# Products made two groups ahead of an engine's other steps, in the local stage of a four-block model

## The reference

```python
x = x + attn_a(layernorm(x))   # local: 16 heads of 16, each query sees 44 fixed offsets
x = x + ffn(layernorm(x))      # 8 groups of 512 tokens, two linear maps, no activation
x = x + attn_b(layernorm(x))   # full attention over 2 x 2048 tokens, rotary q and k
x = x + ffn(layernorm(x))
```

```python
k_mod = k[:, :, idx] * (1.0 + scale_embed)            # idx = t - offset, 0..40, 128, 96, 384
scores = einsum('bhtd,bhtjd->bhtj', q, k_mod) / sqrt(HD) + pos_bias    # masked where idx < 0
attn = softmax(scores)
out = einsum('bhtj,bhtjd->bhtd', attn, v[:, :, idx]) * if_gain
```

## Time and profile before

| | us |
|---|---|
| median of 3 runs | 2927.61 |
| lowest and highest | 2920.57, 2934.63 |
| the profiled execution | 2935.33 |
| its span | 2933.7 |

### The profile page before, as it was taken

The page is one execution under the profiler, slowest core; times in us unless marked ns, Lnnn a source line. Parts: engine busy times, 40 slices in busy tenths (PEclk is TensorE's granted clock), DMA queues, the critical chain, the costliest instruction groups (busy, mean ns, idle before and its releaser), DMA issues. The chain is left out here.

```text
span 2933.7 us, 50620 instructions
## 1 busy us (share of the span) xinstructions
PE 2547.2 (87%) x15600; PEld 1009.9 (34%) x15600; DVE 2106.6 (72%) x3525; ACT 1382.5 (47%) x1695; POOL 736.7 (25%) x971
## 2 busy tenths in 40 slices
PE   7678788788887756799899899898999999999787
PEld 5334444444443431233232233232233333323233
DVE  4376767767777536588788788788888888888323
ACT  0133333333333310466566566566666666666611
POOL 0487655656665202400200201002000000000000
PEclk9799899989998885899999999999999999999999
DMA  7324434334334326900400402204000000000042
GB/s 229 115 61 109 112 88 120 95 98 127 79 102 126 99 75 98 100 7 15 54 7 19 50 4 40 29 7 61 4 15 11 8 19 8 7 19 7 22 157 97
DMA packets 243735, 183.54 MB, mean 63 GB/s; under 512 B 103172, under 2 KB 212373, under 8 KB 243605
## 3 DMA queue, kind: packets, MB, share of 16 engines
q1 hardware_dynamic: 209366, 115.80, 14.7%
q0 software_dynamic: 15936, 45.64, 9.4%
q10 hardware_dynamic: 18306, 20.59, 2.2%
HBM read 120.44 MB, written 52.77 MB: 59 GB/s over the span
## 5 line engine op out<-in xcount | busy, mean ns | idle before, releaser
L1172 DVE TENSOR_REDUCE mx<-ps_m 128x1 f32<-128x512 f32 x2064 | 1301.1, 683 | 285.4 <-PE ps_m L1034 276.8
L1158 ACT ACTIVATE pr<-ps_s 128x1024 f32<-128x1024 f32 x1024 | 995.1, 1021 | 604.4 <-PE ps_s L1092 604.0
L1034 PE MATMUL ps_m<-ks,qs 96*128 (+1 forms) x2064 | 723.0, 393 | 46.9 <-DMA qs<-q_d 28.2
L1092 PE MATMUL ps_s<-qs,ks 99*128 (+1 forms) x2048 | 616.2, 382 | 62.1 <-POOLq L968 29.2
L1062 PE MATMUL ps_o<-pr,vg 128*32 128x512 f32 x4104 | 551.2, 609 | 0.6 <-ACT pr L1158 0.6
L515 POOL TENSOR_TENSOR prod_p<-qT,kT 128x512 f32<-128x512 f32 x336 | 412.8, 1259 | 53.6 <-ACT qT L700 22.8
L1034 PEld LDWEIGHTS ps_m<-ks,qs 96*128 (+1 forms) x2064 | 162.3, 97 | 653.6 <-DVE mx L1172 306.9
L978 POOL DMA_DIRECT2D o_d<-on x34 | 18.7, 551 | 1289.4 <-DVE on L1182 1252.1
L1092 PEld LDWEIGHTS ps_s<-qs,ks 99*128 (+1 forms) x2048 | 196.3, 98 | 307.4 <-issue 91.2
L559 PE MATMUL PSa<-prod_p,sj 128*32 128x512 f32 x672 | 211.5, 633 | 71.1 <-ACT sc L712 28.3
L559 PE MATMUL PSa<-prod_d,sj 128*32 128x512 f32 x736 | 211.6, 630 | 69.2 <-DVE prod_d L768 37.8
(11 more groups left out here) (140 smaller groups left out, 2312.7 us busy)
## 6 DMA issues: line engine op xcount, KB each, us to landing
own<-skew SPq DMA_DIRECT2D x64, 512.0 KB
ks<-k_d POOLq DMA_DIRECT2D x42, 256.0 KB, 8.9
qs<-q_d POOLq DMA_DIRECT2D x168, 64.0 KB, 8.9
skew<-attn SPq DMA_DIRECT2D x64, 164.0 KB, 4.3
o_d<-on POOLq DMA_DIRECT2D x34, 256.0 KB, 2.3
w<-in_W SPq DMA_DIRECT2D x8, 1024.0 KB
w<-in_W2T SPq DMA_DIRECT2D x8, 1024.0 KB
vb_d<-vb SPq DMA_DIRECT2D x8, 1024.0 KB, 4.4
```

The lines of the kernel that those rows point to most:

```text
L1034: pe.matmul(ps_m[:, pos % 3, :], qs[0:KROWS, bass.ds(nq, 1), j, qt * P:(qt + 1) * P].rearrange("p a t -> p (a t)"), ks[0:KROWS, bass.ds(ns ...
L1092: mm = pe.matmul(ps_s[:, pair, jj, :], ks[:, bass.ds(slot, 1), j, kk * P:(kk + 1) * P].rearrange("p a t -> p (a t)"), qs[:, bass.ds(q, 1), ...
L1158: act.activation(pr[:, kk % 2, 2 * pair:2 * pair + 2, :], ps_s[:, pair, :, :], ACT.Exp, scale=HD ** -0.5).then_inc(p_ready, 1)
L1172: return dve.tensor_reduce(mx[:, j * TILES + qt, kc:kc + 1], ps_m[:, pos % 3, :], AX_X, ALU.max).then_inc(m_read, 1)
```

## The change

VectorE and GpSimd make, in slot s, the products of slot s+2 (`LEAD`), and then take the slot's other steps; VectorE's wait for constants moves to slot -2 with them. TensorE still takes the products of slot s in slot s, but in every fourth slot, where a new bank begins, it does its other steps first. The first "q" of a chunk moves one slot forward. The rings stay at 6.

```diff
+LEAD = 2
-    (-7, "h_normalise", 0), (-6, "k", 0), (-5, "k", 1), (-3, "q", 0), (1, "v", 0), (3, "v", 1), (6, "q", 1),
+    (-7, "h_normalise", 0), (-6, "k", 0), (-5, "k", 1), (-4, "q", 0), (1, "v", 0), (3, "v", 1), (6, "q", 1),
...
@@ GpSimd
-                if 0 <= slot < NG * SLOTS:
-                    products(slot // SLOTS, slot % SLOTS)
+                if 0 <= slot + LEAD < NG * SLOTS:
+                    products((slot + LEAD) // SLOTS, (slot + LEAD) % SLOTS)
...
@@ TensorE
-                if 0 <= slot < NG * SLOTS:
+                late = slot % 4 == 0
+                if 0 <= slot < NG * SLOTS and not late:
                     products(slot // SLOTS, slot % SLOTS)
                 for j, what, i in steps_in(slot):
                     step(j, what, i)
+                if 0 <= slot < NG * SLOTS and late:
+                    products(slot // SLOTS, slot % SLOTS)
...
@@ VectorE
-                if slot == 0:
+                if slot == -LEAD:
                     dve.wait_ge(filled, 6)
                     dve.wait_ge(const_ld, 16 * N_CONST)
-                if 0 <= slot < NG * SLOTS:
-                    products(slot // SLOTS, slot % SLOTS)
+                if 0 <= slot + LEAD < NG * SLOTS:
+                    products((slot + LEAD) // SLOTS, (slot + LEAD) % SLOTS)
```

## The result

| | before | after |
|---|---|---|
| median of 7 runs, us | 2927.84 | 2949.41 |
| lowest and highest | 2920.57, 2934.63 | 2940.96, 2952.96 |
| span of the profiled execution | 2933.7 | 2947.8 |
| its mean granted clock | 0.930 | 0.929 |

The ratio is 1.0063, 95% interval 1.0049 to 1.0076: the changed kernel is slower by 0.6%, some 18 us (21.6 by the medians). I had forecast 2911 us, 0.6% faster. The time lies at the upper end of the range, the sign is wrong, and the price is that of the rival "the ring behind the late slot 16" (2945 us).

A forecast was written before the change was run, and what follows sets the result against it. No engine is full in the local stage; TensorE's waits for VectorE and ScalarE bound it. Six periods of 3.5 gained less 1.6 lost, plus 5 in the fill, give 16.4 us off 2927.6: 2911 us, range 2870 to 2950.

The forecast's parts named there:

- the ring behind the late slot 16: Slot 16: VectorE waits for score matmuls put behind "h_back" and two "values"; slower, 2945 us; chance 0.16.
- What bounds the stage: Local stage, 128 to 968 us: no engine is full; TensorE's waits before its score matmuls, together 137 us, are the target.
- Half A: Chunk from "k" to the end of "qk", 76.2 us before: 3.5 us gained, ends 1 and 6.
- Half B: Chunk from the end of "qk" to the next "k", 39.8 us before: 1.6 us lost, ends 1.2 gained and 4.7 lost.
- GpSimd's burst: Half B, six GpSimd products in a row, 8.27 us, slowing VectorE's operations beside them; 1.0 us taken as freed.
- put on the rival: Clock rival: fewer but longer TensorE waits, each followed by 6.8 us more at half clock; slower, 2952 us; chance 0.08.
- my end of 4.7: From "qk" to the next "k": the losing end, 4.7 us lost, with "k" at values + 20.6.
- The rule of shared ports: VectorE with two SBUF inputs and GpSimd reading SBUF exclude each other for a whole instruction; up to 1.3 us each.
- The fill: From 128 to 256 us, where GpSimd sets the pace: 5 us gained, between 0 and 14.
- The sum: Whole kernel: (3.5 - 1.6) x 6 + 5 = 16.4 us gained; the tail after slot 192 has no products.
- The signs: Right: no score bank wait, new "pv" and "turn" waits, period near 114 us; wrong: period under 110 or over 117.
- threshold: Slot 16's products first used later than about 10.9 us after "values" starts (9.0 + 1.9 net) decides the sign.

## Why the prediction was wrong

**What bounds the stage.** That was read rightly: the waits of the earlier trace rows went, and the period is set by TensorE meeting VectorE. It held so well that the regular chunk did not move at all.

**Half A.** Forecast 3.5 us gained, ends 1 and 6; measured 76.2 - 71.6 = 4.6. The half clock after slot 4's update is gone as forecast, and "pv" waits for the mask add: 2.6, 1.7 and 2.0 us in slots 20, 5 and 8, where I had 2.4, 1.2 and 1.6. Before "turn" it waits 0.5 and 0.2 us in slots 3 and 9, where I had 1.4 and 1.9; that is most of what half A gained over the forecast. After the last "pv" of these of them stands a new 3.4 us at half clock (558.8), half of what I had feared for the lower end.

**Half B, the positions.** Forecast: "values" at qk + 23.9, VectorE's held product 9.0 us later, by its terms the mask add ended at values + 14.2 (9.0 + 0.6 + 2.8 + 1.25 + 0.55), "k" at values + 17.5. Measured: 595.73 - 570.30 = 25.4; 8.8; 14.0; 18.9. The mechanism was told rightly down to the instruction, and two terms were mis-sized. The first is the 1.0 us taken as freed from GpSimd's burst: nothing was freed, since a GpSimd that is held by its ring starts its burst later and not never, and it fell beside the next operations of the same kind. I had asked where GpSimd would stop, not where it would go on. The second is the clock: TensorE's wait of 4.62 us (I had 3.3) is followed by 3.3 us with a granted clock of 0.52, close to its lower level of 1.2 GHz, which I had put on the rival and not into the sum. Together half B lost 4.5 us where I had 1.6, near my end of 4.7.

**The rule of shared ports.** I weighed the Trainium skill (SBUF — State Buffer, "SBUF: two separate sides"), by which the two engines exclude each other for a whole instruction, and gave a freed operation up to one product. In the regular chunk the trace agrees, with 1.46 and 1.76 us. In the fill it does not stop at one: 6.33 us, until five products of GpSimd had passed. The measurement decides, and in the fill this is worth some 4 us that I had not in the sum.

**The fill.** Forecast 5 us gained, between 0 and 14; measured, from the first product to the copy of chunk 2's "k", 9.4 us lost. This is the step that failed most, and its range had no side below zero. The argument "GpSimd sets the pace, so little comes back" treated a lead as something that can only be worth less than hoped. Of the 9.4, 3.0 are lost up to chunk 1's copy (56.4 us against 53.4) and 6.4 between the two copies (88.4 against 81.9). The first part is no larger than what GpSimd's lead costs there: without it in chunk 0 the copy comes 4.1 us earlier, though with ring 8 and both leads it also comes 2.4 earlier. The second part is the ring's: the trace has VectorE held for 7.63 us and GpSimd for 9.16 up to 247 us by their rings; with ring 8 the two copies are 82.5 us apart, and without GpSimd's lead in chunk 0 still 88.5. Slot 16 is not what costs here (87.4 without it). With the waits came more half clock, 34.4 us up to chunk 2's copy in place of 20.4, which can be up to 7 of the 9.4 us (an estimate: 14 us at half speed); no run separates the clock from the waits that it follows.

**The sum.** It took the six periods as alike. Measured: the fill loses 9.4 us; of the five periods between the copies of chunk 2 and chunk 7, four lose 0.2 us together and one 3.7; and from that copy to the last score matmul 3.9 us are lost. Less the 0.6 by which the products start earlier, this makes the 16.6 us. The long chunk has the same 8.2 us of waiting before "values" as its neighbours, but then 13.6 us at half clock in place of 10.2, and VectorE's product held for 10.0 us in place of 7.5: that is near my end of half B, the late work all at half clock, in one chunk. The last chunk has 27.2 us at half clock in place of 20.4. Why just these two stays open. Of the 30.5 us between the forecast 16.4 gained and the 14.1 lost in the span, the fill has 14.4, the two halves of six regular chunks 10.8 (1.9 forecast, 0.1 measured), and these two chunks nearly all of the rest. The tail behind the products, which I had put at nothing, cost nothing (16.6 us late at its start, 16.4 at its end).

**The signs.** Of those that I had named as right, the score bank's wait is gone but for 0.4 us a chunk and the low clock after slot 4 altogether, and the new waits before "pv" and "turn" are there; VectorE's wait in slot 16 was 7.5 us and not 4, the wait before "values" 8.2 and not 6 to 7, the period 116.0 and not 114. The sign of being wrong also came: VectorE's subtractions beside GpSimd got slower on average (991 ns from 860).

**The ring rival.** It named the mechanism, the place, the instructions queued behind and the half B price (4.7 against 4.5). I gave it 0.16, because its threshold, first use 10.9 us after "values", stood above my 9.0, and 8.8 it was. But the threshold was 9.0 plus the 1.9 net of a chunk, and the net was 0.1 at 8.8 us, which puts it at 8.9, and with a fill that loses lower still. A threshold inherits the errors of every other term of its sum. The run with slot 16 not late shows this slot's price: 2.4 us a chunk on average in the stretch that the rival named. The rival had the fill at 5 us gained like the forecast, so its 2945 us came near the measured time partly by luck: it put half A at 1 us gained, where 4.6 were, and six chunks at 22 us lost, where 7.8 were; that the fill lost 9.4 made up for it.

**What the forecast never asked** is how the two parts act on each other. I costed them as one. Priced one at a time, each would have come out faster (measured 0.9% and 0.8%), and the question would have been what the late slot does to the ring that the lead has filled.

## What to carry to other kernels

Running a producer ahead uses up the slack of its ring: before adding a lead, count for each product which use frees its buffer, and add a buffer where that use falls in the slots that the lead spans (here 7 for 6, 48 us). Do not combine a producer that runs ahead with a consumer that is put late, without that buffer. A producer that shares a port and runs ahead makes more products before it turns to its next other step; look for the short operation of a critical chain that stands beside such a run, and count what is left of the run when that operation is due.

## What the hardware showed unexpectedly

VectorE's subtraction of 128 x 352 from SBUF operands was held in the fill until the end of GpSimd's run of products, in the traces of all sixteen kernels: always ending 0.4 us behind the run, and lasting as long as the run still had to go. It took 2.88 us before, 6.33 after and 7.74 with ring 8. The length of the run does not give this time: beside 17 products it took 2.88, 3.17 and 3.18 us, but 4.56 with the late slots alone, where VectorE came to it earlier, and beside 31 unbroken products (before, ring 8) 2.89. In the regular chunks of the kernel after it took 1.6 us at most, though often more products followed. Why it gets in there and not in the fill stays open. I did not try to keep these operands out of SBUF.
